# Gated delta rule on one core: one fp32 residual step for the block inverse, full-size matmuls in place of 64x64 ones, and new engine orders

## What is computed

```
A = -where(strict_tril, einsum('bhnce,bhnde->bhncd', k_beta, kc) * decay, 0.0)
T = solve_triangular(eye - A, eye, lower=True)
value_ = T @ v_beta
k_cumdecay = T @ (k_beta * exp(g)[..., None])
# step, chunk after chunk
v_new = v_i - kcd_i @ state
out_i = (q_i * exp(g_i)) @ state + attn @ v_new
state = state * exp(g_last) + (k_i * exp(g_last - g_i)).T @ v_new
```

## Time and profile before

| | us |
|---|---|
| median of 3 runs (lowest, highest) | 5349.92 (5344.38, 5359.94) |
| profiled execution, first to last instruction | 5350.3 |
| PE busy | 4982.9 (93%) |
| DVE busy | 4483.8 (84%) |
| ACT busy | 4371.8 (82%) |
| POOL busy | 2064.9 (39%) |

### The profile page before, as it was taken

The page is one execution under the profiler, slowest core; times in us unless marked ns, Lnnn a source line. Parts: engine busy times, 40 slices in busy tenths (PEclk is TensorE's granted clock), DMA queues, the critical chain, the costliest instruction groups (busy, mean ns, idle before and its releaser), DMA issues. The chain is left out here.

```text
span 5350.3 us, 132947 instructions
## 1 busy us (share of the span) xinstructions
PE 4982.9 (93%) x38788; PEld 3326.6 (62%) x38788; DVE 4483.8 (84%) x9152; ACT 4371.8 (82%) x9744; POOL 2064.9 (39%) x1433
## 2 busy tenths in 40 slices
...
DMA packets 185165, 377.26 MB, mean 71 GB/s; under 512 B 86400, under 2 KB 95744, under 8 KB 184960
## 3 DMA queue, kind: packets, MB, share of 16 engines
...
## 5 line engine op out<-in xcount | busy, mean ns | idle before, releaser
L653 PE MATMUL p_proj<-hid,w_in 128*128 128x512 f32 x3072 | 1620.5, 610 | 32.4 <-POOL ident L1163 29.7
L998 DVE SCALAR_TENSOR_TENSOR conv<-pre,taps,conv 128x512 f32<-128x512 f32 x1536 | 1207.8, 793 | 41.9 <-ACT conv L857 37.6
L911 ACT ACTIVATE x_bd<-x_t 64x512 bf16<-64x512 bf16 x1280 | 804.5, 629 | 215.7 <-DVE x_t L1079 198.9
L1205 POOL TENSOR_TENSOR o_sc<-o_sc,neg_half 128x8 f32<-128x8 f32 x128 | 268.6, 2099 | 1622.0 <-DVE o_sc L1135 1622.0
L653 PEld LDWEIGHTS p_proj<-hid,w_in 128*128 128x128 f32 x3072 | 496.6, 192 | 64.5 <-POOL ident L1163 30.0
L838 PE MATMUL p_out<-h_t,w_out 128*128 128x512 f32 x1024 | 501.9, 613 | 0.8 <-DVE h_t L1140 0.8
L1072 DVE TENSOR_TENSOR y_h<-p_lev,y_h 128x512 bf16<-128x512 f32 x640 | 441.3, 690 | 44.2 <-PE p_lev L707 37.9
L1116 DVE TENSOR_TENSOR vw<-p_b,w_c 128x256 f32<-128x256 f32 x384 | 156.9, 409 | 378.8 <-PE p_b L796 378.8
L1079 DVE STREAM_TRANSPOSE x_t<-y_h 128x512 bf16<-128x512 bf16 x640 | 454.6, 710 | 19.3
L1064 DVE TENSOR_TENSOR q_h<-p_lev,consts 128x512 bf16<-128x512 f32 x640 | 438.6, 685 | 37.9 <-PE p_lev L701 33.3
L1172 POOL TENSOR_TENSOR low<-g_row,consts 128x1024 f32<-128x1024 f32 x128 | 302.1, 2360 | 410.1 <-ACT dec L895 409.9
...
## 6 DMA issues: line engine op xcount, KB each, us to landing
w_in<-in_w_in SPq DMA_DIRECT2D x128, 768.0 KB, 6.2
g_row<-rows_scratch SPq DMA_DIRECT2D x128, 512.0 KB, 3.1
hid<-h_scratch SPq DMA_DIRECT2D x128, 512.0 KB, 7.3
e_row<-exp_rows_scratch SPq DMA_DIRECT2D x128, 512.0 KB, 5.1
w_out<-in_w_out SPq DMA_DIRECT2D x128, 256.5 KB, 2.6
...
```

The source lines that it names most:

```text
L653: last = pe.matmul(p_proj[tile % 2][:], w_in[p][:, kt, tile * P:(tile + 1) * P], hid[p][:, kt, :], start=(kt == 0), stop=(kt == KT - 1))
L911: last = act.activation(x_bd[block, :, block], x_t[block], ACT.Copy)
L998: dve.scalar_tensor_tensor(conv[:, tile, :], pre[:, tile, j:j + S], taps[p][:, tile, j:j + 1], conv[:, tile, :], ALU.mult, ALU.add).then_i ...
```

## The change

The inverse is refined once instead of twice: the residual R = ga x y is formed in fp32 from a copy of the approximate inverse widened to fp32 (y_full), the identity is added (resid), and the result is W = x_dn + (R as an upper bf16 part and a rest r_lo) x x_dn + R_upper x (R_upper x x_dn). The upper bf16 part isn't copied: it is read in place as every second 16-bit word of the fp32 tile. The three 64x64 matmul stages read zero-padded tiles at full size. Steps AD, AL, d, N, n, E, e go; AO (ACT), YW and RL (POOL), F0, F1 (DVE), G0, G1 (PE) and v0, v1 (ACT) come; AB0 and AB1 read the fp32 ga. All four orders are new. The waits on the shared PSUM banks are written for the new order; they aren't shown.

```diff
-PE_ORDER = ("Z6@1 P9@2 D0@1 XC@1 D1@1 ON0@0 N0@1 ON1@0 P10@2 N1@1 KK0@2 KK1@2 P11@2 E0@1 P0@3 W0@1 E1@1 TR0@1 "
-            "P1@3 U0@1 O0@1 L@2 W1@1 KS1@1 P2@3 M1@2 TR1@1 Y1@2 U1@1 O1@1 M2@2 P3@3 KS2@1 VT0@2 Y2@2 VT1@2 TR2@1 "
-            "P4@3 M3@2 P5@3 U2@1 Y3@2 O2@1 M4@2 OY0@0 KS3@1 P6@3 Y4@2 TR3@1 QT@3 M5@2 O3@1 P7@3 Y5@2 P8@3 Q6@2 "
-            "KT@3 XD@2 OY1@0")
-ACT_ORDER = ("Z0@2 Z1@2 e0@1 IV0@1 AD@2 VX0@1 e1@1 SV1@2 OT0@1 C0@3 XB1@2 SV0@2 VX1@1 XB2@2 IV1@1 OT1@1 C1@3 OQ0@1 "
-             "XB3@2 VX2@1 VK0@2 C2@3 VK1@2 OT2@1 XB4@2 OQ1@1 SQ@3 VX3@1 OQ2@1 XB5@2 OT3@1 OQ3@1 SK@3 QN@3 C3@3 "
-             "KT@3 XD@2 KN@3 YC@2 d0@2 d1@2 XC@2 GE@3")
-DVE_ORDER = ("VW0@1 AB0@2 AB1@2 T8@2 ST0@1 y0@2 X1@2 RR1@1 q1@2 VW1@1 y1@2 X2@2 ST1@1 q2@2 RR2@1 y2@2 X3@2 VW2@1 "
-             "T3@3 q3@2 T4@3 y3@2 T5@3 X4@2 ST2@1 q4@2 T0@3 RR3@1 YA0@0 y4@2 SN1@2 X5@2 T1@3 q5@2 T2@3 y5@2 s10@2 "
-             "s11@2 SN0@2 OS0@1 OS1@1 T6@3 p6@2 QN@3 SN2@2 T9@3 YA1@0 KN@3 T7@3 T10@3 HT0@1 T11@3 n0@2 HT1@1 SM0@3 "
-             "SM1@3 SM2@3 n1@2 SM3@3 GA0@3 GA1@3 GA2@3 GA3@3")
-POOL_ORDER = ("OP@0 ON@0 PW@2 GL@3 SL@2 SD1@1 QD@2 SD2@1 AL@2")
+PE_ORDER = ("P11@2 G0@1 P0@3 W0@1 G1@1 P1@3 TR0@1 L@2 P2@3 U0@1 M1@2 P3@3 KS1@1 O0@1 Y1@2 VT0@2 TR1@1 M2@2 W1@1 U1@1 "
+            "P4@3 Y2@2 KS2@1 O1@1 M3@2 VT1@2 TR2@1 P5@3 U2@1 Y3@2 O2@1 KS3@1 P6@3 M4@2 TR3@1 P7@3 Y4@2 O3@1 M5@2 "
+            "OY0@0 QT@3 Y5@2 P8@3 KT@3 Q6@2 XD@2 OY1@0 Z6@2 P9@3 ON0@1 ON1@1 P10@3 D0@2 D1@2 KK0@3 XC@2 KK1@3")
+ACT_ORDER = ("v0@1 Z1@2 IV0@1 SV0@2 SV1@2 C0@3 v1@1 VX0@1 XB1@2 OT0@1 C1@3 AO@2 XB2@2 VX1@1 OQ0@1 IV1@1 VK0@2 OT1@1 "
+             "XB3@2 VX2@1 VK1@2 C2@3 OT2@1 XB4@2 VX3@1 OQ1@1 SQ@3 OQ2@1 OT3@1 OQ3@1 XB5@2 SK@3 C3@3 QN@3 KT@3 XD@2 "
+             "KN@3 YC@2 GE@3 Z0@3 XC@2")
+DVE_ORDER = ("GA2@2 GA3@2 T8@2 T11@2 AB0@2 AB1@2 VW0@1 y0@2 X1@2 ST0@1 q1@2 T0@3 RR1@1 y1@2 X2@2 VW1@1 T3@3 q2@2 "
+             "ST1@1 T1@3 y2@2 RR2@1 X3@2 q3@2 VW2@1 T4@3 ST2@1 y3@2 X4@2 RR3@1 T5@3 q4@2 T6@3 y4@2 X5@2 T2@3 q5@2 "
+             "OS0@1 OS1@1 YA0@0 SN0@2 y5@2 s11@2 s10@2 T9@3 SN1@2 p6@2 QN@3 SN2@2 KN@3 YA1@0 T7@3 HT0@1 HT1@1 T10@3 "
+             "F0@2 SM0@3 SM1@3 F1@2 SM2@3 SM3@3 GA0@3 GA1@3")
+POOL_ORDER = ("RL@1 SL@2 QD@1 SD1@1 GL@3 SD2@1 OP@1 ON@1 YW@2 PW@3")
...
+        def top(ap):
+            return ap.bitcast(BF)[:, 1::2]
+
+        def tops(ap):
+            return ap.bitcast(BF)[:, :, 1::2]
...
                 elif name == "Q":
...
-                        last = pe.matmul(p_lev[HB:P, u * HB:(u + 1) * HB], a_d[0:HB, u, HB:P], y_h[0:HB, u, :],
-                                         start=True, stop=True)
+                        last = pe.matmul(p_lev[:, u * HB:(u + 1) * HB], a_off[:, u, :], y_h[:, u, :], start=True, stop=True)
...
                 elif name == "D":
+                    t.wait(pe, "y_wide")
+                    t.wait(pe, "strict")
...
-                        pe.matmul(bank(n)[:, u - n * 4, :], a_d[:, u, :], y_dn[:, u, :], start=True, stop=False)
-                        last = pe.matmul(bank(n)[:, u - n * 4, :], a_lo[:, u, :], y_dn[:, u, :], start=False, stop=True)
+                        last = pe.matmul(bank(n)[:, u - n * 4, :], ga[p][:, u, 0, :], y_full[:, u, :], start=True, stop=True)
...
+                elif name == "G":
+                    t.wait(pe, "r_done", n + 1)
...
+                        last = pe.matmul(bank(n)[:, u - n * 4, :], top(resid[:, u, :]), x_dn[:, u, :], start=True, stop=True)
...
                 elif name == "W":
+                    t.wait(pe, "g_done", n + 1)
+                    t.wait(pe, "rlo")
...
-                    pe.matmul(p_out[n][:], ident3[:], quarter(x_dn, n).rearrange("p a i -> p (a i)"),
+                    pe.matmul(p_out[n][:], ident_h[:], quarter(x_dn, n).rearrange("p a i -> p (a i)"),
...
-                        pe.matmul(bank(n)[:, u - n * 4, :], f0[:, u, :], x_dn[:, u, :], start=False, stop=False)
-                        last = pe.matmul(bank(n)[:, u - n * 4, :], f1[:, u, :], x_dn[:, u, :], start=False,
+                        pe.matmul(bank(n)[:, u - n * 4, :], r_lo[:, u, :], x_dn[:, u, :], start=False, stop=False)
+                        pe.matmul(bank(n)[:, u - n * 4, :], top(resid[:, u, :]), x_dn[:, u, :], start=False, stop=False)
+                        last = pe.matmul(bank(n)[:, u - n * 4, :], top(resid[:, u, :]), g_t[:, u, :], start=False,
...
-                elif name == "AD":
+                elif name == "AO":
                     t.wait(act, "strict")
...
+                    act.activation(a_off[0:HB, :, HB:P], ga[p][0:HB, :, 0, HB:P], ACT.Copy).then_inc(s["aoff"], 1)
...
+                elif name == "v":
+                    t.wait(act, "g_mm", n + 1)
...
+                    act.activation(quarter(g_t, n), bank(n), ACT.Copy).then_inc(s["g_done"], 1)
...
                 elif name == "AB":
-                    t.wait(dve, "ad")
+                    t.wait(dve, "strict")
                     t.wait(dve, "q_mm", back=1)
-                    dve.tensor_copy(a_bd[half(n), :, half(n)], a_d[half(n), :, half(n)]).then_inc(s["abd"], 1)
+                    dve.tensor_copy(a_bd[half(n), :, half(n)], ga[p][half(n), :, 0, half(n)]).then_inc(s["abd"], 1)
...
+                elif name == "F":
+                    t.wait(dve, "d_mm", n + 1)
...
+                    dve.tensor_tensor(quarter(resid, n), bank(n), each(const["ident"], 4), ALU.add).then_inc(s["r_done"], 1)
...
+                elif name == "YW":
+                    t.wait(pool, "y21")
+                    t.wait(pool, "ydn")
...
+                    pool.tensor_copy(y_full[:], y_dn[:]).then_inc(s["y_wide"], 1)
+                elif name == "RL":
+                    t.wait(pool, "r_done")
...
+                    pool.tensor_tensor(r_lo[:], resid[:], tops(resid[:]), ALU.subtract).then_inc(s["rlo"], 1)
```

More of the change, by code:

```diff
@@ L733, in emit @@
                     t.wait(pe, "xdn")
-                    pe.sem_inc(passed, 1)
                     for u in range(U):
-                        last = pe.matmul(p_tr[0:HB, u * HB:(u + 1) * HB], y_dn[HB:P, u, 0:HB], ident_h[HB:P, HB:P],
-                                         start=True, stop=True)
+                        last = pe.matmul(p_tr[:, u * HB:(u + 1) * HB], y_dn[:, u, :], ident_h[:, HB:P], start=True, stop=True)
                     last.then_inc(s["xt7"], 1)
                 elif name == "D":
-                    t.wait(pe, "y21")
@@ L759, in emit @@
                     for u in range(n * 4, n * 4 + 4):
-                        last = pe.matmul(bank(n)[:, u - n * 4, :], x_dn[:, u, :], f0[:, u, :], start=True, stop=True)
-                    last.then_inc(s["n_mm"], 1)
-                elif name == "E":
-                    t.wait(pe, "n_done", n + 1)
-                    t.wait(pe, "strict")
+                        last = pe.matmul(bank(n)[:, u - n * 4, :], top(resid[:, u, :]), x_dn[:, u, :], start=True, stop=True)
+                    last.then_inc(s["g_mm"], 1)
+                elif name == "W":
+                    t.wait(pe, "g_done", n + 1)
+                    t.wait(pe, "rlo")
```

134 lines of the change are left out of this document (70 added, 64 removed).

## The result

The changed kernel takes 5746.4 us (5742.8 to 5756.9, 4 runs) against 5350.2 (5344.4 to 5359.9, 4 runs) before: ratio 1.0744, 95% interval 1.0729 to 1.0759. The forecast was 5785 (5080 to 5980), slower with a chance of 0.71.

The account below looks back on a forecast made before the run. No engine was full; engines waiting for each other in fixed order set the period. DVE's 33.65 plus gaps gave 35.0, plus port waits 2.0, 1.1, 2.5, 1.9 gave 42.5 against 39.09, times 128 iterations +435: 5785 us (5080 to 5980).

Parts of the forecast that it names:

- DVE's own work: DVE's work per iteration without waiting for SBUF, the floor of the period: 33.65 us.
- its gaps: DVE's dependency gaps 0.6, y5's wait 0.3, SM chain 0.4, KN 0.1; PE's own waits said to lie inside 42.5.
- (a): On DVE, SM3 behind F1 waits for POOL's RL to release SBUF, and all GA wait for SM3: 2.0 us.
- (b): After GA3, T8 on DVE holds POOL's SL, then SL holds T11: 1.1 us.
- (c): On DVE, AB0 and AB1 each stand behind a half of POOL's QD: 2 x 1.27 = 2.5 us.
- (d): POOL's ON starts in front of T9 and SN1, which stand before p6 on DVE: 1.90 us.
- T0 behind GL: On DVE, T0 beside POOL's GL: 0 to 2.4 us, taken as nothing and kept for the range.
- rival (4): New orders avoid the port, but PE's every-second-word weights run at fp32's spacing: +1.3 on PE, 37.6, 5158 us; chance 0.04.
- Rival (1): AB on DVE does not use the shared port and costs 0.68 each: 40.5, 5531 us; chance 0.10.
- Rival (5): POOL's PW holds the port as long as it runs, T10 waits up to 1.5: 44.0, 5977 us; chance 0.04.
- Rival (2): DVE and POOL waits partly slip past each other, about half of 7.5 left: 39.1, 5350 us, no change; chance 0.09.
- Rival (3): New orders avoid the port as the old did: 36.3, 4992 us, if port waits stay under 4.1; chance 0.18.

Follow-up runs that it names:

- run 6: The changed kernel, orders kept, with POOL's RL, SL, QD, GL, ON and YW working on one column of each block only: 4868.6 us.
- Run 2: The changed kernel with QD moved from behind SL to behind SD2, nothing else: 5288.0 us, ratio 0.9883 to the kernel before.
- run 10: The changed kernel with only SN1 and SN2 moved behind YA1 and T7 behind HT1: 5580.0 us, ratio 1.044 to the kernel before.
- run 9: The changed kernel with SM2, SM3 in front of F1, QD behind SD2, and SN1, SN2 and T7 behind HT1: 5036.4 us.
- run 1: The changed kernel with SM2 and SM3 moved in front of F1, nothing else: 5588.0 us, ratio 1.0444 to the kernel before.

## Why the prediction was right, and where not

Step by step, in us per iteration:

| step | forecast | measured |
|---|---|---|
| DVE's own work | 33.65 | 33.6 |
| its gaps | 1.4 | 2.2 |
| (a) SM3 behind RL | 2.0 | 0.9 |
| (b) T11 behind SL | 1.1 | 0.8 |
| (c) AB behind QD | 2.5 | 2.0 |
| (d) SN1 behind ON | 1.9 | 1.7 |
| T0 behind GL, T7 behind YW | 0 (0 to 3.5) | 1.0 (T0 0.8, T7 0.14) |
| period | 42.5 | 42.3 |

- **The floor.** 33.65 came out to the hundredth (run 6), and it holds in all edits of the change up to 0.4, J's own run left aside. The sum of rows of the kernel before was good here because no DVE instruction but AB changed its duration (F takes 0.68 as n did), and AB's cast from fp32 is 0.42 unheld, as taken from L372.
- **(a)** was mis-sized: its working, 2.14 - 0.1 = 2.0, took RL at AL's length (RL is 1.89) and took for certain what 0.1 us in RL's start decides. SM3 is held 1.7 in every second iteration.
- **(b), (c), (d)** happened where and for the reason I said, and were 0.2 to 0.5 smaller. For (c) I took two whole halves of QD for AB, but AB0 comes to the port 0.5 us after the first has begun, and AB1 0.35 after the second (2632.46 behind 2631.97, 2633.98 behind 2633.63).
- **T0 behind GL** I took as nothing and kept for the range. T0 took 2.94 us in 29 of the 80 iterations, 0.8 more on average. All 29 are iterations in which PE's clock had fallen, so this term seems to hang on (c). Run 2 ends it, and run 10 ends it with QD left where it is.
- **The gaps** were 0.8 too small, and the statement that PE's own waits lie inside the 42.5 is the step that failed: in 64 of the 80 iterations PE's clock fell at its stand for AB1, and DVE then waited 0.93 us before ST0, for U0. In the 16 with the same stand and full clock that wait is not there, nor is it in experiment 2.
- **PE.** D's 16 fp32 instructions took 2.0 us (forecast 1.9), a full small stage 0.23; weights read as every second word cost nothing. PE's timeline in W of the changed kernel, two of every three reading resid in place:

```profile
2630.35 0.22 PE L794 MATMUL p_out<-x_dn,r_lo 128*128 128x128 bf16 x1
2630.41 0.22 PE L795 MATMUL p_out<-x_dn,resid 128*128 128x128 bf16 x1
2630.47 0.22 PE L796 MATMUL p_out<-g_t,resid 128*128 128x128 bf16 x1
```

  They start 0.06 apart, as those of the earlier trace rows: rival (4) is out. **ACT** gave back 1.5 (forecast 1.6).
- **Rival (1)** (AB off the port) is out: 1.43 beside QD, 0.42 beside nothing. **Rival (5)** is out as well: YW and PW stay at 1.04 and 2.08, and a tap that starts inside PW takes 0.74 (the kernel before has one wholly inside it), so PW shuts nobody out. The Trainium skill's page "SBUF — State Buffer" ("Who interferes with whom") has the lock last for the whole instruction; the trace agrees for RL, QD, ON, SL, GL and YW, whose victims get through only as these end, and not for PW.
- **Rival (2)**, that the waits partly slip past each other, is out: 6.4 of held time were there, where it has half of 7.5. **Rival (3)**, 36.3 us and 4992, is out for the change, but its figure for the new orders without port waits was near: run 9 reaches 36.6 with 0.9 still held, and run 6 has 35.4 with nothing held. Its point, 4.1 us of port waits, lies where the runs have it: run 2 with 3.6 is faster than before, runs 10 and 1 with 4.6 and 5.1 are not.

That the sum came within 0.3 us of the measured period is partly luck: 1.1 too much in (a) and 0.9 too much in (b) to (d) together stand against 1.0 of T0 and T7 and 0.8 of gaps that I had not in the sum.
